# A two-layer perceiver block on one core: the first cross attention with a folded weight product and deeper context buffers, unrolled normalisations, and p.v of the second cross attention in 32-column tiles

## The reference, cut to what matters

```python
# layer 0, cross attention with one head of width 512
xn = layernorm(x)
q = xn @ L0_xattn_Wq + L0_xattn_bq            # per batch element: 32 rows
k = ctx @ L0_xattn_Wk + L0_xattn_bk           # 257 rows
v = ctx @ L0_xattn_Wv + L0_xattn_bv
x = x + softmax(q @ k.T * 512**-0.5) @ v
# layer 1, cross attention with 16 heads of width 32
q, k, v = heads(xn @ W_Q + b_Q), heads(ctx @ W_K + b_K), heads(ctx @ W_V + b_V)
x = x + (softmax(q @ k.T * 32**-0.5) @ v) @ W_O + b_O
```

## Time and profile before

| | us |
|---|---|
| median of 3 runs | 2329.41 |
| lowest and highest run | 2316.37, 2331.72 |
| profiled execution | 2322.6 |
| its span on the core | 2320.8 |
| PE busy in it | 2001.2 (86%) |

### The profile page before, as it was taken

How to read it: one execution, slowest core, us unless ns; L and a number is a source line. 1 busy time by engine, 2 the same in 40 slices (tenths; PEclk the granted TensorE clock), 3 DMA queues, 4 the chain that set the end, 5 groups by cost and what they waited for, 6 DMA issues and landing times. The chain is left out here.

```text
span 2320.8 us, 41841 instructions
## 1 busy us (share of the span) xinstructions
PE 2001.2 (86%) x15348; PEld 1726.6 (74%) x15348; DVE 1043.7 (45%) x1881; ACT 943.3 (41%) x1575; POOL 922.1 (40%) x657
## 2 busy tenths in 40 slices
PE   5896899945999994699999999878847999999993
PEld 4543677735999993688888888756637999999993
DVE  4135262545655557333333333355643454454442
ACT  2111151512666662233333333225514555555551
POOL 2000332103777776333333332222105666666653
PEclk9897889965999997799999999979878999999997
DMA  3394001013888887311111101010016665666663
GB/s 132 114 354 141 26 17 55 2 37 140 277 281 277 278 278 233 111 37 28 37 32 32 36 27 36 1 46 23 3 37 218 216 215 197 219 211 197 224 195 118
DMA packets 102157, 298.13 MB, mean 128 GB/s; under 512 B 10896, under 2 KB 27920, under 8 KB 102064
## 3 DMA queue, kind: packets, MB, share of 16 engines
q1 hardware_dynamic: 76624, 231.83, 29.9%
q0 software_dynamic: 11840, 38.81, 5.4%
q10 hardware_dynamic: 13600, 26.22, 3.0%
HBM read 264.32 MB, written 32.51 MB: 128 GB/s over the span
## 5 line engine op out<-in xcount | busy, mean ns | idle before, releaser
L133 PE MATMUL banks<-ra 128*128 128x256 f32 (+4 forms) x3004 | 983.5, 328 | 42.6 <-DVE ra L1025 10.4
L134 PE MATMUL banks<-ra 128*128 128x256 f32 (+4 forms) x3004 | 968.3, 323 | 0.0
L135 PE MATMUL banks<-ra 128*128 128x256 f32 (+4 forms) x3004 | 965.4, 322 | 0.0
L133 PEld LDWEIGHTS banks<-ra 128*128 128x128 f32 (+2 forms) x3004 | 579.3, 193 | 101.5 <-DVE ra L1025 16.3
L135 PEld LDWEIGHTS banks<-ra 128*128 128x128 f32 (+2 forms) x3004 | 578.7, 193 | 43.5
L134 PEld LDWEIGHTS banks<-ra 128*128 128x128 f32 (+2 forms) x3004 | 580.1, 193 | 35.9
L1480 POOL TENSOR_TENSOR ra<-fa,ra 128x1024 fp32r<-128x1024 f32 x187 | 446.4, 2388 | 237.1 <-ACT ra L1513 236.1
L1513 ACT ACTIVATE ra<-fa 128x1536 fp32r<-128x1536 f32 x190 | 281.5, 1483 | 85.2 <-DMA fa<-in_L_units 67.9
L1597 DVE TENSOR_TENSOR ra<-fa,ra 128x256 fp32r<-128x256 f32 x190 | 162.5, 855 | 92.0 <-ACT ra L1537 92.0
L331 POOL TENSOR_TENSOR ra<-fa,ra 128x2048 fp32r<-128x2048 f32 (+2 forms) x22 | 85.6, 3904 | 297.2 <-ACT ra L325 289.2
L1572 DVE TENSOR_TENSOR ra<-fa,ra 128x512 fp32r<-128x512 f32 x190 | 133.5, 703 | 115.8 <-ACT ra L1513 109.0
(11 more groups left out here) (225 smaller groups left out, 2270.7 us busy)
## 6 DMA issues: line engine op xcount, KB each, us to landing
fa<-in_L_units SPq DMA_DIRECT2D x190, 768.0 KB, 4.5
fa<-in_ctxT SPq DMA_DIRECT2D x64, 514.0 KB, 4.8
ea_y_scratch<-fa ACTq DMA_DIRECT2D x35, 512.0 KB, 4.4
fa<-in_ctx SPq DMA_DIRECT2D x32, 512.0 KB, 5.8
eb_y_scratch<-fa ACTq DMA_DIRECT2D x15, 512.0 KB, 3.6
fa<-in_L_attn_w_qkvT SPq DMA_DIRECT2D x6, 1024.0 KB, 7.7
normed_scratch<-na SPq DMA_DIRECT2D x16, 256.0 KB, 2.1
x<-in_x SPq DMA_DIRECT2D x1, 2048.0 KB, 8.3
```

The lines of the kernel that those rows point to most:

```text
L133: pe.matmul(psum, lh, rh, start=first, stop=False)
L134: pe.matmul(psum, lh, rl, start=False, stop=False)
L135: return pe.matmul(psum, ll, rh, start=False, stop=last)
```

## The change

In stage A, M = Wq.Wk^T is computed once (48 matmuls) from the transposed weights, in a first block that also loads `x`, makes the constants, does the normalisation and rounds Wv; q' = xn.M + `through_k` follows in a second block (96 matmuls). `u_row` (12 matmuls) and `away` on DVE give the `shift`. Two buffers each hold `ct`, `cn` and `cl`; tile 0 is loaded in the first block, tile 1 in the second, and in the loop tile n+2 when tile n has been used. The loop nests of `scores` and `p_ctx` are interchanged, so that the four elements follow one another inside each chunk. `nb`'s gain and bias are loaded at the start of stage A's last block. `layer_norm` is unrolled, uses four buffers always, and without gain gives every second tile to ACT. In stage D `p_v` computes the diagonal blocks only, as 32 matmuls of 128x32 weights with 32 columns, and DVE adds them at once.

```diff
+                    def _(eng):
+                        eng.dma_start(staging[0], columns(d["L0_xattn_WqT"])).then_inc(s_wq, 16)
+                        eng.dma_start(staging[1], columns(d["L0_xattn_WkT"])).then_inc(s_wk, 16)
+                        eng.dma_start(x[:], d["x"].rearrange("(t p) d -> p t d", p=P)).then_inc(s_x, 16)
+                        eng.dma_start(staging[2], columns(d["L0_xattn_Wv"])).then_inc(s_wv, 16)
+                        load_turned(eng, 0, 0)
+                        eng.wait_ge(s_ql, 1)
+                        eng.wait_ge(s_kl, 1)
+                        load_rows(eng, 0, 0)
...
+                        eng.wait_ge(s_vh, 1)
+                        pool.tensor_tensor(wv[1], staging[2], wv[0].bitcast(F32), ALU.subtract).then_inc(s_vl, 1)
...
+                        for c in range(DC):
+                            cols = slice(c * P, (c + 1) * P)
                             for k in range(DC):
+                                ins = mm3(banks[:, MB + c, :], wq[0][:, k, cols], wq[1][:, k, cols], wk[0][:, k, :], wk[1][:, k, :],
+                                          k == 0, k == DC - 1)
+                            ins.then_inc(s_fold, 1)
...
+                        for j, (h, c) in enumerate(jobs):
+                            eng.wait_ge(s_mm, j + 1)
+                            dve.tensor_scalar(qp[:, c, h * HALF:(h + 1) * HALF], banks[:, MB + j % 4, :], through_k[:, c:c + 1],
+                                              None, ALU.add).then_inc(s_out, 1)
...
+                            links.link(dve.scalar_tensor_tensor(away, x[:, j, :], moments[:, j, 0:1], u_row, ALU.subtract,
+                                                                ALU.mult))
+                            links.link(dve.reduce_sum(shift[:, j:j + 1], away, AX_X))
...
+                        with eng.Fori(0, NT // 2 - 1) as i:
+                            for u in range(2):
+                                n = 2 * i + u
+
+                                eng.wait_ge(s_sc, SEQ * n + 3 * SEQ)
+                                load_turned(eng, n + 2, u)
+
+                                eng.wait_ge(s_pv, SEQ * n + 2 * SEQ)
+                                load_rows(eng, n + 2, u)
...
                             for c in range(DC):
-                                ins = pe.matmul(banks[NQ * j:NQ * j + NQ, u, 0:S], qg[u][:, c, NQ * j:NQ * j + NQ],
-                                                ct[j][:, c, :], start=c == 0, stop=c == DC - 1)
-                            ins.then_inc(s_sc, 1)
...
+                                for j in range(SEQ):
+                                    ins = pe.matmul(banks[NQ * j:NQ * j + NQ, u, 0:S], qg[u][:, c, NQ * j:NQ * j + NQ],
+                                                    ct[u][j][:, c, :], start=c == 0, stop=c == DC - 1)
...
-                        o = chunks(banks[:, T1, :])
-                        for h in range(4):
-                            rows = slice(XD * h, XD * h + XD)
-                            ins = dve.tensor_tensor(ot[rows, :, NQ * j:NQ * j + NQ], o[rows, :, rows], o_last[rows], ALU.add)
-                        ins.then_inc(s_o, 1)
+                        o = banks[:, T1, 0:P].rearrange("p (i q) -> p i q", i=DC)
+                        dve.tensor_tensor(ot[:, :, NQ * j:NQ * j + NQ], o, o_last, ALU.add).then_inc(s_o, 1)
...
-                        for c in range(DC):
-                            cols = slice(c * P, (c + 1) * P)
+                        for i in range(DC):
                             for k in range(2):
-                                ins = pe.matmul(banks[:, T1, cols], v[u][:, k, cols], pt[:, k, cols], start=k == 0,
-                                                stop=k == 1)
+                                for c in range(DC):
+                                    own, cols = slice(XD * c, XD * c + XD), slice(i * P + XD * c, i * P + XD * c + XD)
+                                    ins = pe.matmul(banks[own, T1, i * NQ:(i + 1) * NQ], v[u][:, k, cols], pt[:, k, cols],
+                                                    start=k == 0, stop=k == 1)
```

In `layer_norm`, the core of what changes for ACT (the loops over tiles are written out, for all engines):

```diff
+            def by_scalar(n):
+                return not affine and n % 2 == 1
...
+                    for n in range(NT):
+                        eng.wait_ge(s_turned, n + 1)
+                        act.activation(xh[:, :, n * P:(n + 1) * P], chunks(banks[:, n % L, :]), ACT.Copy).then_inc(s_hi, 1)
+                        if n + L < NT and by_scalar(n + L):
+                            normalise(n + L)
+                        if ahead and n == NT // 2 - 1:
+                            programs, loads, splits = ahead
+                            programs[1](eng, splits[:1])
```

More of the change, by code:

```diff
@@ L187, in _ @@
                 def _(eng):
-                    if ahead and rows is not None:
+                    if ahead:
                         programs, loads, splits = ahead
@@ L191, in _ @@
                     if rows is not None:
+                        for n in range(NT):
+                            wait_normed(eng, n)
+                            eng.dma_start(rows.rearrange("(t p) d -> t p d", p=P)[n], xn[n % L]).then_inc(s_rows[n % L], 16)
                         for u in range(L):
[L193 to L206, removed]
+                            eng.wait_ge(s_rows[u], 16 * (NT // L))
                 @block.gpsimd
@@ L266, in _ @@
-                    for u in range(L):
-                        low_part(NT - L + u, u)
+                    for n in range(L):
+                        if not by_scalar(n):
+                            normalise(n)
+                    for n in range(NT):
+                        if n + L < NT and not by_scalar(n + L):
+                            normalise(n + L)
+                        eng.wait_ge(s_hi, n + 1)
+                        own = slice(n * P, (n + 1) * P)
+                        dve.tensor_tensor(xl[:, :, own], chunks(banks[:, n % L, :]), xh[:, :, own].bitcast(F32),
+                                          ALU.subtract).then_inc(s_lo, 1)
@@ L347, in cross_one_head @@
+            cl = [f.take(D) for _ in range(2)]
             f3 = f.at
-            wv = r.take(DC, D), r.take(DC, D)
-            bk_parts = r.take(DC, 2)
-            r2 = r.at
-            wq, wk = (r.take(DC, D), r.take(DC, D)), (r.take(DC, D), r.take(DC, D))
-            q = [r.take(DC, HALF) for _ in range(2)]
-            load, high, low, s_w = split_programs("xa", [
-                (*wq, columns(d["L0_xattn_Wq"])), (*wk, columns(d["L0_xattn_WkT"])),
-                (*wv, columns(d["L0_xattn_Wv"]))], staging)
@@ L356, in cross_one_head @@
-            s_ctxT = [sem(f"xa_ctxT{j}") for j in range(SEQ)]
-            s_sc, s_bk = sem("xa_scores"), sem("xa_bk_split")
-            def load_turned(eng, n):
-                for j in range(SEQ):
-                    if not (isinstance(n, int) and n == 0):
-                        eng.wait_ge(s_sc, SEQ * n + (SEQ + 1 + j))
-                    eng.dma_start(ct[j], d["ctxT"][SEQ * n + j]).then_inc(s_ctxT[j], 16)
-            layer_norm("na", ahead=((load, high, low), (0, 1, 2), (0,)))
-            s_b, s_mm, s_hi, s_out = sem("xa_biases"), sem("xa_product"), sem("xa_high"), sem("xa_taken")
```

746 lines of the change are left out of this document (416 added, 330 removed).

## The result

The changed kernel takes 2266.4 us (median of 4 runs, 2265.4 to 2270.2) where the kernel before takes 2328.6: a ratio of 0.9745, 95% interval 0.9714 to 0.9777. It is 62 us faster; forecast were 70, from 2329 to 2259. The profiled execution of the changed kernel took 2267.15 us; its span is 2264.7.

The account below looks back on a forecast made before the run. It took a waiting start-up and two loops nearly filled by PE, stage A's also near the DMA's limit, as the bound. Stage A -49, normalisations -2 and stage D -19 made -70: 2252.6 profiled, 2259 median, range 2240 to 2283.

Parts of the forecast that it names:

- Start-up: Stage A before the first scores: they start at 72.5 us instead of 90.6, -18, bounds -24 and -12.
- Loop of A: Stage A's tile loop becomes DMA-bound at 11.3 us a tile: -31 of the -49 forecast for all of A.
- then one p.ctx of 3 and the tail, 13: End of stage A: after transfers finish at 145.7, only these 3 and 13.0 us follow, ending the stage at 161.7.
- bound of 9.8 a tile: Stage A's loop: what PE alone would need per tile, the better bound, -39 us for the loop.
- rival (c): Stage A: DMA gives no more than today, 12.27 us a tile, start-up at its worse bound; 2270 us, chance 8%.
- Normalisations: The five normalisation blocks: `nb` -3 for its bias wait, small shifts elsewhere; sum -2 us, bounds -6 and +3.
- +0.8 for `nd` and `ne`: Normalisations ahead of stages D and E: POOL or ACT's own chain ends the block, each about 0.8 us later.
- Stage D: Heads' cross attention: p.v shorter, 0.5 us less a step, and 0.9 gained where a tile ends; -19, bounds -21 and -5.
- cap of 0.58 on a step's gain: Stage D: at most 0.58 us of p.v's gain counts, since the third key product waits for ACT's copy.
- (b): Stage D: p.v gains nothing, as a column group loads its next weights only after its last matmul; 2273 us, 12%.
- (d): Stage D: p.v's 64 records pass one at a time, at 0.11 us each; slower, 2446 us, chance 4%.
- rule of 62 ns a record: Trainium skill page's sequencer time per MATMUL: stage D's p.v would take 4.0 us, the kernel 2348; the prediction doubted it.

Follow-up runs that it names:

- lighter load: Changed kernel, but stage A's loop loads only a quarter of each context row's columns for p.ctx; 2262.3 us, ratio 0.9722, stage A 173.0.
- second pair of profiles: Kernel before and changed kernel each profiled once more, unedited, on one chip; spans 2327.2 and 2265.7 us, changed kernel's ratio 0.9727.
- the experiment: Changed kernel with the four plain normalisations all on DVE, none on ACT, still unrolled; 2264.4 us, ratio 0.9733.
- combined kernel: Changed kernel with earlier transposes, ACT's key copy between exponentials, normalisations ahead of D and E on DVE, Wv's preparation under the product block; 2236.6 us, ratio 0.9620.

## Why the forecast held, and where it failed

**Start-up, right in its sum.** PE began at 12.9 instead of 10.5, M was done at 28.5 instead of 27, the product block began at 44.1 instead of 42.5 plus the block change, the scores at 71.97 instead of 72.5. The two terms said to be covered by nothing (Wv's 1.90 and 3.81) showed in full. That the sum is within 0.5 owes something to luck: the last transposes were rounded at 37.9 instead of 35, and from the product block's start to the scores were 27.9 instead of 30. And the -18 were taken from a profile whose start-up ran at a low clock (90.6, where the second had 86.4).

**Loop of A, the step that failed.** Forecast -49 for the stage, measured -34.2 and -33.2. Of the 14.8 between 161.7 and 176.5:
- 3.3: the second half of tile 2's loads was issued at 86.8 instead of 83.5, since the first scores and p.ctx ran at half the clock (0.61 from 72 to 88).
- 1.6: from there the transfers took 63.8 (86.8 to 150.6) instead of 62.2. The rate was as estimated, but not for the reason given. The lighter load kept 11.2, and the earlier transposes made it 10.5: PE's order and clock had a part in it that the sum did not have.
- 9.9: the step "then one p.ctx of 3 and the tail, 13". It let the last p.ctx start when its rows landed. In the code's order the p.ctx and the values of earlier tiles and a copy by DVE come first, and it started 8.1 later (158.7); it then ran at half the clock and took 4.8, 1.8 more. The tail was 13.0 as forecast. With the transposes one tile earlier the stage ends 13 sooner.

The bound of 9.8 a tile was thus not reached even with a light load, and rival (c), 12.27 a tile, did not occur either. "The DMA above 0.97 busy" and "PE waiting for context loads" were seen, and still did not show that the transfers alone set the pace: the lighter load was needed for that.

**Normalisations, too small.** Forecast -2, measured -6.1 over the five blocks, -4.4 in the second pair of profiles (`nb` -4.2, `nc` -1.4). `nb` gave 4.7 (28.73 to 24.07 us from its first aggregate to the next product), not 3, and `nc` 2.6, not 0.5: I had costed the passes moved to ACT and the load of the gain, and left out the unrolling with four buffers. For `nc` the experiment shows that it is this; for `nb` no run parts it from the load. The +0.8 for `nd` and `ne` were +0.75 and +0.72.

**Stage D, right in kind, mis-sized twice.** p.v was costed at 1.2, by the nearest row of another tile form; it is 0.56 from first to last start, so the step saves 0.98 and not 0.5. Of that 0.24 went into the wait for ACT's key copy that the text named: 0.74 a step. Where a tile ends, 0.9 were gained as forecast, but the wait of 1.09 only went to 0.84, not to a few tenths: p.v ends earlier too, and DVE's add then stands behind the reciprocal that waits for ACT's exponentials. 24 x 0.74 + 8 x 0.92 = 25, measured 23 to 24 with `nd`'s +0.75 inside. The cap of 0.58 on a step's gain was too low: it took the moment of the copy as given by the exponentials, but the earlier trace rows show it waiting 0.16 for PE's first key product, and this comes earlier too when p.v is shorter; 0.58 + 0.16 is the 0.74 measured.

**The rivals.** (b) priced a group at one record in 110 ns, the duration of a load in the earlier trace rows. A group gives one in 27 ns on its own, with loads that the trace still shows as 114 ns long, so that the duration was no measure of the rate. Only on one group after another is p.v as long as before (1.84 to the next product, where it was 1.80). (d), records one at a time at 53 ns or more, and the rule of 62 ns a record: 9 ns.

**The comparison with one profile.** The 7 us between profile and median of the kernel before were added as if they spread evenly. They are of the size of stage E's two lengths, 188.1 in that profile and 196.6 in the next; that this explains them was not shown.

## What to carry to other kernels

When a loop is expected to become bound by its transfers, add what stands in program order between the last landing and the end of the last tile; that is where a third of this forecast's loop gain went. Small matmuls with 32 columns of weights belong on the four column groups in turn, since one group by itself starts a record every 27 ns and four in turn every 9. A stage that did not change and yet differs by several us should be profiled again before it is explained.

## What the runs showed of the hardware that was not expected

- 64 records with 128x32 weights and 32 columns start within 0.56 us, 9 ns apart, if four column groups take turns, and within 1.71, 27 ns apart, on one group after another.
- With the lighter load, idle times of 0.8 to 1.5 us ahead of p.ctx, tile after tile, were in places followed by half the clock (p.ctx 3.62 and 3.64 instead of 1.93) though PE was busy for 52.1 of 60 us. With the transposes earlier, and so one wait a tile behind a long product, the clock stayed up from 108 us to the stage's end; in the combined kernel, with the same order, it was 0.79 from 155 on.
- The same code on the same inputs ran stage E in 188.1 or 196.6 us, by whether the clock fell at the start of a product or behind it.
- With its loads issued without delay one core drew 395 GB/s from 98 to 140 us (4.2 MB in 10.5), where the changed kernel drew 370.
